# A split matrix product on one core: a head tile first, a ring of 18 tiles in shrinking pieces, and a register-addressed TensorE loop

## What is computed

```python
entities = jnp.einsum('be,le->bl', entity_idxs, W)      # 1024 x 12500 times 12500 x 128
s = jnp.sum(entity_idxs, axis=1)
s_safe = jnp.where(s != 0, s, 1.0)
scale = jnp.where(s != 0, 1.0 / s_safe, 1.0)
return entities * scale[:, None]
```

## Time and profile before

| | us |
|---|---|
| median of the runs (lowest, highest) | 151.04 (150.97, 151.16) |
| the profiled execution: its time | 151.15 |
| its span | 149.4 |
| TensorE matmul busy in the span | 135.2 (91%) |
| VectorE, ScalarE busy | 94.5, 84.1 |
| mean rate of all transfers | 390 GB/s |

### The profile page before, as it was taken

How to read it: one execution, slowest core, us unless ns; L and a number is a source line. 1 busy time by engine, 2 the same in 40 slices (tenths; PEclk the granted TensorE clock), 3 DMA queues, 4 the chain that set the end, 5 groups by cost and what they waited for, 6 DMA issues and landing times.

```text
span 149.4 us, 2230 instructions
## 1 busy us (share of the span) xinstructions
PE 135.2 (91%) x785; PEld 76.4 (51%) x785; DVE 94.5 (63%) x110; ACT 84.1 (56%) x129; POOL 0.7 (0%) x13
## 2 busy tenths in 40 slices
PE   0597998799999999999999999999999999999960
PEld 0244654455555555555555655655555555665530
DVE  0471953746756845955954954864864778965593
ACT  3571852735735834844843854763763677955173
POOL 1000000000000000000000000000000000000000
PEclk9999999999999999999999999999999999999998
DMA  5999999999999999999999999999999999999022
GB/s 147 404 427 459 405 454 399 449 420 425 444 410 449 410 444 420 434 434 410 454 415 434 420 439 429 410 459 410 434 425 439 408 425 416 414 406 342 16 70 75
DMA packets 5719, 58.19 MB, mean 390 GB/s; under 512 B 638, under 2 KB 1534, under 8 KB 2514
## 3 DMA queue, kind: packets, MB, share of 16 engines
q1 hardware_dynamic: 5714, 58.13, 92.6%
HBM read 57.60 MB, written 0.52 MB: 389 GB/s over the span
## 4 chain that ended last, share of the span: by engine, by line
DMA 56%; PE 35%; DVE 4%; SPq 1%; issue 1%
DMA xw<-main 56%; PE acc L417 35%; DVE y_sum L366 2%; DVE low_max L320 1%; SPq L167 1%; DVE row_sum L363 0%; SPq L163 0%; SPq L165 0%; DVE row_sum L357 0%; DVE row_sum L360 0%; DVE any_low L396 0%; PE acc L470 0%; DVE inexact L398 0%
## 5 line engine op out<-in xcount | busy, mean ns | idle before, releaser
L417 PE MATMUL acc<-parts_main,xw 128*128 128x385 bf16 x640 | 108.2, 327 | 3.8 <-DMA xw<-main 3.0
L417 PEld LDWEIGHTS acc<-parts_main,xw 128*128 128x128 bf16 x640 | 61.3, 98 | 50.7 <-issue 8.4
L320 DVE TENSOR_REDUCE low_max<-xw 128x2048 uint16 x20 | 45.5, 2278 | 0.0
L243 ACT ACTIVATE parts_main<-xw 128x512 bf16<-128x512 bf16 x20 | 12.7, 635 | 47.0 <-DMA xw<-main 37.7
L309 DVE TENSOR_TENSOR w_rest<-xw 128x512 f32<-128x512 f32 x20 | 13.8, 692 | 40.0 <-DMA xw<-main 40.0
L250 ACT ACTIVATE act_out<-xw 128x2048 bf16<-128x2048 uint16 x20 | 37.9, 1893 | 0.0
L316 DVE TENSOR_TENSOR parts_main<-w_rest 128x512 bf16<-128x512 f32 x21 | 14.6, 695 | 0.7
L246 ACT ACTIVATE parts_main<-w_rest 128x512 bf16<-128x512 bf16 x21 | 13.3, 635 | 2.0
L417 PE MATMUL acc<-parts_short,xw_short 84*128 84x385 bf16 x8 | 2.7, 522 | 5.5 <-ACT parts_short L246 5.5
L320 DVE TENSOR_REDUCE low_max<-xw_taper 128x1 f32<-128x1024 uint16 (+1 forms) x6 | 6.1, 1038 | 1.4 <-DMA xw_taper<-ends 1.3
L250 ACT ACTIVATE act_out<-xw_taper 128x1024 bf16<-128x1024 uint16 (+1 forms) x6 | 5.4, 906 | 1.7 <-DMA xw_taper<-ends 1.6
(11 more groups left out here) (50 smaller groups left out, 38.2 us busy)
## 6 DMA issues: line engine op xcount, KB each, us to landing
xw<-main SPq DMA_DIRECT2D x20, 2304.0 KB, 16.3
xw_taper<-ends SPq DMA_DIRECT2D x2, 1024.0 KB, 24.9
x_final<-ends SPq DMA_DIRECT2D x3, 512.0 KB, 27.8
xw_taper<-ends SPq DMA_DIRECT2D x1, 1408.0 KB, 21.8
xw_ramp<-ends SPq DMA_DIRECT2D x1, 1280.0 KB, 7.5
xw_taper<-ends SPq DMA_DIRECT2D x1, 1280.0 KB, 18.8
xw_taper<-ends SPq DMA_DIRECT2D x2, 512.0 KB, 27.1
xw_ramp<-ends SPq DMA_DIRECT2D x1, 704.0 KB, 4.9
```

The lines of the kernel that those rows point to most:

```text
L243: nc.scalar.activation(parts[0:rows, 0:n, 0:L], top(words, n), ACT.Copy)
L320: nc.vector.tensor_reduce(low_max[0:rows, bass.ds(col, 1)], low(words, n), AX.XY, ALU.max).then_inc(dve_checked, 1)
L417: return nc.tensor.matmul(acc[:, b, 0:N], x, parts, start=first, stop=last)
```

## The change

- **Pieces.** The first load is a head tile with its x, its W, the W of the first three tiles of the loop and of the first three of the last six. The short tile is second. Then 90 tiles go through a ring of 18 tile places, in 33 pieces of 3 or 4 tiles first, then 3, 2, and 1. Each tile row holds its own x and the W of a tile three later. The last 6 tiles (before: 4) come by pairs of banks in `FINAL`. Loads are 41 (before: 35). The slow path's buffers are `kept`.
- **Units.** VectorE and ScalarE work in units of 3 tiles (30 units, six slots of `parts`).
- **A counter.** Each piece has a semaphore of its own. GpSimd waits for them in order and adds the piece's number of tiles to `landed`, on which the other engines wait.
- **TensorE's loop.** Two nested loops (5 rounds, 6 slots) run one body of 24 matmuls. The addresses of x and of the parts come from registers, and each tile has its own wait for `landed`.
- **The end.** The checks of the last pieces are split one quarter to VectorE, three to ScalarE; two banks are summed in one instruction; the last bank is scaled by VectorE instead of ScalarE, with a semaphore of its own, `y_last_ready`.

The diff, cut to its core. The slow path, which doesn't run here, and the placing of the data in memory are left out.

```diff
-T = 4
-SLOTS = 4
-MAIN = 20
-RAMP_X = (1, 2)
-RAMP_W = (3, T)
-TAPER_X = (2, 2, 2, 2, 1, 1)
-TAPER_W = (T, 6, 0, 0, 0, 0)
-LAST = 4
-
-FINAL = ((0, 2, 0, 4), (2, 4, 0, 4), (4, 6, 0, 4), (6, 7, 0, 4), (7, 8, 0, 2), (7, 8, 2, 4))
-TILES = sum(RAMP_X) + MAIN * T + sum(TAPER_X)
...
+UNIT = 3
+SLOTS = 6
+RING = SLOTS * UNIT
+ROUNDS = 5
+UNITS = ROUNDS * SLOTS
+LOOP = UNITS * UNIT
+PIECES = (3, 3, 4, 4, 4,
+          4, 4, 4, 3, 3,
+          4, 4, 4, 3, 3,
+          3, 3, 3, 3, 2, 2, 2,
+          2, 2, 2, 2, 2, 2, 2, 1, 1, 1, 1)
+
+LAST = 6
+FINAL = ((0, 2, 0, 6), (2, 4, 0, 6), (4, 6, 0, 6), (6, 7, 0, 6), (7, 8, 0, 4), (7, 8, 4, 6))
+
+PAIRS = ((0, 2), (2, 4), (4, 6), (6, 7), (7, 8))
+
+ALONE = LAST - UNIT
+
+KEPT = 4
...
+        xw = sb("xw", [P, RING, ROW], F32)
+        xw_head = sb("xw_head", [P, B + (1 + UNIT + ALONE) * L], F32)
...
-        parts_b = sb("parts_b", [P, TAPER_W[1], N], BF16)
+        parts = sb("parts", [P, SLOTS, UNIT, N], BF16)
+        parts_alone = sb("parts_alone", [P, ALONE, N], BF16)
...
-        taper_in = [sem(f"taper_in_{k}") for k in range(NT)]
+        piece_in = [sem(f"piece_in_{k}") for k in range(len(PIECES))]
+        landed = sem("landed")
...
+            for k, n in enumerate(PIECES):
+                pool.wait_ge(piece_in[k], 16)
+                pool.sem_inc(landed, n)
+
...
-            def load_main(m, s):
-                sp.dma_start(xw[:, s, :], main[m]).then_inc(main_in[s], 16)
-
-            sp.dma_start(xw_short[0:short, :], piece(0)).then_inc(short_in, 16)
-            for k in range(NR):
-                sp.dma_start(xw_ramp[k][:, :], piece(1 + k)).then_inc(ramp_in[k], 16)
-            for s in range(SLOTS):
-                load_main(s, s)
-            with sp.Fori(1, MAIN // SLOTS) as i:
-                for s in range(SLOTS):
-                    m = SLOTS * i + s
-                    sp.wait_ge(products_done, m - SLOTS + EDGE + 1)
-                    sp.wait_ge(dve_checked, m - SLOTS + EDGE + 1)
-                    sp.wait_ge(act_checked, m - SLOTS + EDGE + 1)
-                    load_main(m, s)
-            for k in range(NT):
-                sp.dma_start(xw_taper[k][:, :], piece(1 + NR + k)).then_inc(taper_in[k], 16)
+            sp.dma_start(xw_head[:, :], edge(0)).then_inc(head_in, 16)
+            sp.dma_start(xw_short[0:short, :], edge(1)).then_inc(short_in, 16)
+            for k, n in enumerate(PIECES):
+                last_unit = (FIRST_TILE[k] + n - 1) // UNIT
+                if last_unit >= SLOTS:
+                    sp.wait_ge(products_done, used(last_unit - SLOTS))
+                    sp.wait_ge(dve_checked, used(last_unit - SLOTS))
+                    sp.wait_ge(act_checked, used(last_unit - SLOTS))
+                j = FIRST_TILE[k] % RING
+                sp.dma_start(xw[:, j:j + n, :], piece(k)).then_inc(piece_in[k], 16)
...
-                sp.dma_start(x_final[k][:, :], piece(1 + NR + NT + k)).then_inc(final_in[k], 16)
+                sp.dma_start(x_final[k][:, :], edge(2 + k)).then_inc(final_in[k], 16)
...
-                sp.wait_ge(y_ready, b1)
+                if b1 < BANKS:
+                    sp.wait_ge(y_ready, b1)
+                else:
+                    sp.wait_ge(y_last_ready, 1)
                 sp.dma_start(out_pairs[:, b0:b1, :], y[:, b0:b1, :]).then_inc(y_out, 16)
...
+                    u = SLOTS * i + s
+                    act.wait_ge(landed, UNIT * u + UNIT)
+                    act.wait_ge(products_done, used(u + 1 - SLOTS))
+                    split(unit_w(s), parts[:, (s + 1) % SLOTS, :, :], UNIT, (s + 1) % 2, unit_split(u + 1))
+                    act.wait_ge(act_checked, used(u - 2))
+                    low_sum(unit_x(s, B // 2), u + 2, (s + 1) % 2).then_inc(act_checked, 1)
...
+                act.wait_ge(final_in[k], 16)
+                act.wait_ge(act_checked, used(UNITS + k - 2))
+                low_sum(tiles(x_final[k][:, dve_share(k):], 1), 2 + UNITS + k, (k + 1) % 2).then_inc(act_checked, 1)
...
+                    u = SLOTS * i + s
+                    dve.wait_ge(landed, UNIT * u + UNIT)
+                    dve.wait_ge(top_parts_done, unit_split(u - 1))
+                    rest(unit_w(s), UNIT, (s + 1) % 2)
+                    dve.wait_ge(products_done, used(u + 1 - SLOTS))
+                    lo(parts[:, (s + 1) % SLOTS, :, :], UNIT, (s + 1) % 2, unit_split(u + 1))
+                    low_largest(unit_x(s, 0, B // 2), u + 2).then_inc(dve_checked, 1)
...
+            def add_parts(b0, b1):
+                return nc.vector.tensor_reduce(y_sum[:, b0:b1, :],
+                                               acc[:, b0:b1, 0:ONES].rearrange("p b (k l) -> p b l k", k=PARTS),
+                                               AX.X, ALU.add)
...
             def finish(pair):
                 b0, b1 = PAIRS[pair]
-                for b in range(b0, b1):
-                    dve.wait_ge(bank_full, b + 1)
-                    if b == b1 - 1:
-                        row_sum_is_zero(b0, b1, ONES).then_inc(sum_step, 1)
-                    add_parts(b).then_inc(y_summed, 1)
+                dve.wait_ge(bank_full, pair + 1)
+                row_sum_is_zero(b0, b1, ONES).then_inc(sum_step, 1)
+                add_parts(b0, b1).then_inc(y_summed, 1)
...
-            pair = 0
-            for k, (b0, b1, j0, j1) in enumerate(FINAL):
-                check_final(k)
-                if k and FINAL[k - 1][3] == LAST:
-                    finish(pair)
-                    pair += 1
-            finish(pair)
-
-            dve.wait_ge(act_checked, CHECKS)
-            dve.wait_ge(dve_checked, CHECKS)
+            check(0)
+            check(1)
+            finish(0)
+            check(2)
+            finish(1)
+            check(3)
+            check(4)
+            finish(2)
+            check(5)
+            finish(3)
+            finish(4)
+            dve.wait_ge(inverse_done, len(PAIRS))
+            dve.wait_ge(y_summed, len(PAIRS))
+            nc.vector.tensor_scalar(y[:, BANKS - 1, :], y_sum[:, BANKS - 1, :], row_sum[:, BANKS - 1, 2:3], None,
+                                    ALU.mult).then_inc(y_last_ready, 1)
...
-            def multiply(words, n, parts, rows=P, first=False):
-
-                x = top(words, n)
-                for j in range(n):
-                    for b in range(BANKS):
-                        mm = product(b, x[:, j, b * P:(b + 1) * P], parts[0:rows, j, :], first)
-                mm.then_inc(products_done, 1)
-
-            def wait_parts(count):
+            def multiply(x, parts, first=False):
+
+                for b in range(BANKS):
+                    mm = product(b, x[:, b * P:(b + 1) * P], parts, first)
+                return mm
...
+            pe.wait_ge(head_in, 16)
+            wait_split(HEAD_SPLIT)
+            multiply(top(tiles(xw_head[:, 0:B], 1))[:, 0, :], parts_head[:, 0, :], first=True).then_inc(products_done, 5)
...
-            wait_parts(1)
-            multiply(xw_short[0:short, 0:B], 1, parts_short, rows=short, first=True)
-            for k, x in enumerate(RAMP_X):
-                pe.wait_ge(ramp_in[k], 16)
-                wait_parts(2)
-                multiply(xw_ramp[k][:, 0:x * B], x, parts_ramp[:, sum(RAMP_X[:k]):sum(RAMP_X[:k + 1]), :])
-            with pe.Fori(0, MAIN // SLOTS) as i:
-                for s in range(SLOTS):
-                    m = SLOTS * i + s
-                    wait_parts(unit_count(m))
-                    pe.wait_ge(main_in[s], 16 * (i + 1))
-                    multiply(main_x(s), T, parts_main[:, s, :, :])
...
-            for k, (b0, b1, j0, j1) in enumerate(FINAL):
-                pe.wait_ge(final_in[k], 16)
...
+            wait_split(SHORT_SPLIT)
+            multiply(top(tiles(xw_short[0:short, 0:B], 1))[:, 0, :],
+                     parts_short[0:short, 0, :]).then_inc(products_done, 1)
+            x_flat, parts_flat = xw.rearrange("p j f -> p (j f)"), parts.rearrange("p s j f -> p (s j f)")
+            with pe.Fori(0, ROUNDS) as i:
+                with pe.Fori(0, SLOTS) as s:
+                    wait_split(unit_split(SLOTS * i + s))
+                    for j in range(UNIT):
+                        pe.wait_ge(landed, RING * i + UNIT * s + j + 1)
+                        x = top(tiles(x_flat[:, bass.ds(s * (UNIT * ROW) + j * ROW, B)], 1))[:, 0, :]
+                        mm = multiply(x, parts_flat[:, bass.ds(s * (UNIT * N) + j * N, N)])
+                    mm.then_inc(products_done, 1)
...
+            def last_parts(j):
+                return parts_alone[:, j, :] if j < ALONE else parts[:, 0, j - ALONE, :]
...
+            for k in range(NF):
+                pe.wait_ge(final_in[k], 16)
+                for b, mm in last_tiles(k, last_parts, last_product, unit_split(UNITS)):
+                    if b == FINAL[k][1] - 1:
                         mm.then_inc(bank_full, 1)
```

(3 more changed lines are left out.)

393 lines of the change are left out of this document (163 added, 230 removed).

## The result

The changed kernel takes 162.67 us, the median of four runs, against 151.10 for the kernel before: the ratio is 1.076 (95% interval 1.075 to 1.078). Three of the four runs took 162.65, 162.65 and 162.68 us; the fourth took 288.14, counts as slow, is left out of the ratio, and nothing here explains it. It is slower by 11.6 us; I had forecast 146.4 and put the range's end at 160.

A forecast was written before the change was run, and what follows sets the result against it. It took transfers to bound the middle and TensorE, a piece behind its data, the end. From 151.15 us, 3.2 at TensorE's end and 1.4 at the finish gave 146.5, rounded with the runs' median to 146.4; range 144.5 to 160.

The forecast's parts named there:

- the pair is handed over inside the 59 ns gap: TensorE's loop: weight load plus matmul cost the sequencer nothing extra between its own instructions; 3.92 us a unit.
- Rival 1: TensorE's loop: the sequencer becomes the bound because matmuls are not hidden in the gap; 151 to 166.5 us, chance 0.13 plus 0.11.
- 25.15 + 30 u: Whole time in us if the sequencer bounds TensorE's loop, u being a unit's time; decides from u = 4.20 on.
- partly: TensorE's loop: hand-over of matmuls partly adds to the sequencer's time, u = 4.2 to 4.5, 151 to 160 us; chance 0.13.
- fully serial: TensorE's loop: hand-over of matmuls adds in full to the sequencer's time, 4.71 a unit, 166.5 us; chance 0.11.
- the signs named for a sequencer-bound loop: TensorE's loop: loads 0.18 us or more apart in every unit, idle ended by "issue", transfers below full share in the middle.
- Rival 2: TensorE's loop: the sequencer itself does register-addressed matmuls; 8.2 us a unit, 271 us; chance 0.06, including all down to 4.71.
- Middle and start: Main loop bound by transfers, 4.12 us a unit; TensorE starts at 6.75 and its loop at 11.9.
- The end: Final pieces: first lands at 132.5, TensorE's last product at 141.2 against 144.37, 3.2 us won.
- TensorE catches up: Taper: single tiles land every 1.43 us against 1.31 of work, leaving TensorE one or two tiles behind.
- The case of TensorE carrying two tiles: End: TensorE still two tiles behind when the first final piece lands, ending at 141.9 instead of 140.4.
- The finish: After TensorE's last product: VectorE only about 0.3 us behind, span ending at 144.8; 1.4 us won.

The follow-up runs named there:

- experiment 3: The changed kernel with three units (72 matmuls, register addresses kept) in one body of TensorE's inner loop, so fewer turns: 156.99 us, ratio 1.0378.
- experiment 1: The changed kernel with TensorE's inner loop over the six slots written out, matmuls at fixed addresses: 151.85 us, ratio 1.0037.
- experiment 9: The fixed-address version of the changed kernel with ring pieces of 3 and 4 tiles to the end instead of shrinking ones: 151.37 us, ratio 1.0002.
- experiment 11: The fixed-address version of the changed kernel, shrinking pieces, with the slow path and its branch left out of TensorE's program: 148.95 us, ratio 0.9862.
- experiment 12: The fixed-address version with coarse pieces of 3 and 4 tiles, slow path and branch left out of TensorE's program: 151.25 us, ratio 1.0009.
- experiment 6: The kernel before with only the change's finish (quarter checks on VectorE, two banks per sum, last scaling on VectorE): 150.79 us, ratio 0.9971.
- experiment 2: The changed kernel with nested loops and waits kept, but loop matmuls reading the head tile at fixed addresses: 151.03 us, ratio 0.9984.
- experiment 8: The fixed-address version of the changed kernel with 40 of the never-run slow path's last 48 products left out on TensorE: 151.78 us, ratio 1.003.
- experiment 10: The fixed-address version of the changed kernel with 64 semaphore increments ahead of TensorE's first wait, shifting its code: 152.03 us, ratio 1.0056.
- experiment 7: The kernel before with a register-addressed main loop of 32 matmuls a turn and the change's finish: 149.86 us, ratio 0.9926.
- experiment 5: The kernel before with only its main loop changed: register addresses, 32 matmuls a body, a landing counter kept by GpSimd: 150.11 us, ratio 0.9922.

## Why the prediction was wrong, point by point

- **The step that failed** is "the pair is handed over inside the 59 ns gap", which gave 3.92 us for a unit and a chance of 0.59. With registers, computations with a matmul between them mostly start 0.124 to 0.125 us apart, against 46 + 59 = 105 ns: a matmul adds some 20 ns there, and some 50 at one place in each tile. The rest of the sum held: the unit's 34 own instructions last 1.93 us, forecast 1.91 (the address computations 46 ns instead of 50, two of the turn's 110 and 108 instead of 63 each), and at the turn at 84.5 us, where no matmul stands between them, the gaps are 54 to 61 ns. 1.93 + 2.01 = 3.94, and the sequencer comes round every 4.49 or 4.52: the 24 matmuls take 0.55 to 0.58, 23 to 24 ns each, of the 33 that I had as their most. I had called the margin 7 ns a matmul and still taken the free end of it. With both ends unsupported by a row, the sum should have been made at the middle, 4.32 a unit and 154.6, and this alone would have turned the forecast's sign.
- **The pair was not free**: with 27 computations for 24 matmuls each matmul still took 23 to 24 ns of the sequencer's time. The Trainium skill's rule in the prediction ("Advanced Engine Details and Errata", Sequencer Loop), that other instructions can be read and queued while a control instruction executes, doesn't bear the conclusion that I drew beside it.
- **Rival 1 had the mechanism, its place and its formula.** 25.15 + 30 u, with u = 4.50 (4.49 to 4.52) and 0.44 more at each outer turn (4.57 on the mean), gives 162.3; measured 162.67. Near its break-even it gives too little: experiment 3, with a mean of 4.23, would be 152.1, and measured 156.99 less 2.9 for the branch is 154.1; a fast loop stands at landings in the first third, which the formula leaves out (2.9 us in experiment 3). The outer turn's 0.44 was missing in my list, and its value fell between my two cases, partly (to 160) and fully serial (166.5), so that the range ended 2.7 us short.
- **Two of the signs named for a sequencer-bound loop were wrong.** "Issue" ended the idle time, as I had said. But the loads do not stand 0.18 us or more apart through the unit: they stand mostly at the array's 0.164 inside it, and only with the gap at the turn does the mean come to 0.188. And the transfers did not fall below full share in the middle: the ring holds six units, and TensorE was between three and four behind when the loop's last tile landed.
- **Rival 2** (a matmul with register addresses is done by the sequencer, 8.2 a unit) is out: 0.124 for a computation and its pair together.
- **Middle and start held.** The transfers ran at 414 to 440 GB/s in the middle; TensorE started at 6.7 and the loop at 11.92, forecast 6.75 and 11.9.
- **The end held in mechanism, and its data came late.** With fixed addresses the last product is at 143.43, forecast 141.2: 0.9 us won instead of 3.2. "TensorE catches up" held: in experiment 1 it is 0.4 to 0.5 us behind the first two final pieces. The term that was mis-sized is their landing: by the trace the first final piece landed at 135.0 there and at 134.5 in the change, forecast 132.5. I had gone back 7.8 us from 138.3 as the time of the last bytes; they landed at 139.5 in the kernel before, at 140.3 in the change and at 140.7 in experiment 1. About 0.8 us of experiment 1's lateness is the code loaded at 30.7, as the last section shows, which I had kept in the range alone. The case of TensorE carrying two tiles was added up wrongly too: two tiles are 16 x 0.164 = 2.6 us, which gives 143.0 and not 141.9. That small pieces let TensorE approach its data is shown by experiments 9, 11 and 12, 2.3 to 2.5 us.
- **The finish held in size**, 3.75 us behind TensorE's end (forecast 3.6). Its cause was only partly what I wrote: experiment 6 gives the new finish 0.4 of the 1.3 us, and the rest comes with the final pieces of 6 tiles.
- **"The slow path's decision ends sooner than the store's landing, as before"** is true of the change (branch 430 ns) and not of the same kernel with fixed addresses (3236 ns). I had looked at the decision's time and not at the branch behind it.

## What stays open

What decides whether the branch finds its target loaded is not settled. It took 3.2 to 3.6 us in experiments 1, 2, 3, 8 and 10, and 0.34 to 0.46 in all others that have it. Neither a shorter slow path (8) nor a shift by 64 instructions (10) changed it, and experiment 9, with the same TensorE instructions as experiment 1, had it at 0.46. In all seven kernels with a short branch q8 carried 16 KB between 6.6 and 19 us ahead of it; in experiments 1, 2, 3 and 8 it carried nothing between 31 us and the branch. But in experiment 10 it did, at 137.9, and the branch was long all the same. Whether a version with shrinking pieces, fixed addresses and a working slow path on TensorE can keep the 148.95 us of experiment 11 was not tried further; of those that keep the whole slow path, experiment 7 at 149.86 is the fastest.

## What to carry to other kernels

A register-addressed matmul costs TensorE's sequencer an instruction of its own: count them as computation, gap and hand-over, here 0.124 us, or 1.2 for a tile of eight with its longer computations and its wait, plus about 0.85 for a turn with its waits, and compare the sum for a loop body with what the array and the transfers need for it. Here it fits into 5.50 us for 32 matmuls and not into 4.12 for 24. A forecast that hangs on a few ns a matmul, which no row shows, is open in both directions, and its range has to say so. And where a kernel ends with a branch over code that isn't run, look at that branch's own duration in the trace before believing an experiment's total: it hid 2.9 us, and made two different kernels look alike.

## What I had not expected of the hardware

- **A taken branch of 3.2 to 3.6 us.** In experiment 1 the branch over the slow path stood from 146.45 to 149.68. The transfers between 147 and 148 us:

```profile
q8 instruction: 1, 0.02, 7.2%
q14 instruction: 1, 0.01, 2.8%
```

  In experiment 9 a load on the same queue q8 came at 142.1, ahead of the branch, and the branch was short. The Trainium skill, "Runtime: NRT & Kernel Launch", "Instruction fetch mechanics", says that a taken branch whose target isn't in the loaded window forces a fetch before execution goes on. The trace agrees in that a load of 16 KB falls inside the long branches, which last 3.2 to 3.6 us; why the target was not loaded is open, as said above.
- **A load of code can delay data.** The same section calls the cost of crossing from one 16 KB block of the program to the next mostly hidden. Here the program without the load at 24.3 us ended its last product 1.0 us sooner (experiment 5 against before), and one of 16 engines is taken for 1.1 us by it while a landing waits for the last of them. Up to that load the landings of the two stand about 0.1 us apart, and behind it 1.1 to 1.2 to the last main piece. Experiments 1 and 2 show it once more: ScalarE starts on the piece that lands next at 33.44 with the load at 30.7, and at 32.00 without one; the last products end at 143.43 and 142.62. That it is this engine's share that comes last is argued, not shown.
- **The same kind of register computation has several prices on TensorE**: 42 to 51 ns for the addresses, 79 to 84 for the longer ones, and 108 to 110 at the turn; the branch back takes 213.
